# Turning the probabilities of two heads in four: on VectorE in squares of 32 with DMAs, in place of TensorE

## The chip, the cores and the metric

The kernel runs on one core of a Trainium2 chip. The metric is the time of one execution on the device in microseconds (us); below it, one profiled execution is read, in which every instruction of every engine has a start and a duration.

## The reference, cut to what matters

For 8 batches of 512 tokens with 512 features: causal attention with 16 query heads of 128 that share 4 key and value heads, a residual and a layer norm, then a mixture of 8 experts with the best two for each token, a residual and a layer norm. The change touches the attention alone:

```python
q = (x @ wq); k = (x @ wk); v = (x @ wv)          # 16, 4 and 4 heads of 128
scores = scale * q k^T, causally masked
p = exp(scores - row max);  p = p / row sum        # 512 x 512 per head, lower triangle
out = (p @ v) @ wo
x = layernorm(x + out)
```

The product p @ v contracts over keys, so TensorE needs p with the keys on the partitions. The scores come out with the queries there. So p must be turned, head by head.

## The kernel before, in words

The attention is a loop of 32 iterations: `it = 4 b + g`, batch b and key head g, each with the four query heads `n = 4 it` to `n + 3`. An iteration is of a kind: "first" (g = 0, it also makes the batch's values), "group" (g = 1, 2), and "batch" (g = 3, it also turns the next batch's x), or "end" for the last one of all. From the second batch on (`route` true) VectorE also works on the expert choice of a tile of 128 tokens of the batch before.

All engines run the iteration in an order written out by hand (`iteration` in `tensor`, `scalar`, `vector`, `gpsimd` and `sync`), with semaphores that only count up. Each engine is strictly in order, so a wait holds everything behind it. Every matrix product is done in three passes over a high and a low half of its operands; ScalarE copies a result out of PSUM as the high half, and VectorE subtracts this from the result to get the low half. For head n:

- TensorE makes the query (`query`, 12 matmuls) and the scores (`scores`, L1551).
- VectorE takes the scores out with mask and row maxima (`maxima`, L1937), ScalarE takes the exponentials (`exps`, L1824), VectorE inverts the sums (`inverse`, L1945), and GpSimd multiplies (`normalize`, L1423). The result is `probs`, two buffers of 128 x 1280 (the ten 128 x 128 squares on and under the diagonal).
- TensorE turns the ten squares into three PSUM banks (`transposes`, L1574), ScalarE copies these to `pT_hi` (L1834), VectorE makes `pT_lo` (L1948).
- TensorE multiplies with the values, two heads at a time (`values`), and the halves `oT_hi`, `oT_lo` are made by ScalarE and VectorE.
- `out_rows(t)` adds the four heads' part of output tile t, and VectorE's `add_rows` (L1976) takes it from PSUM.

TensorE's order in a group iteration: scores(n+1), out_rows 1 of the iteration before, query 2, turn head n, out_rows 2, turn head n+1, scores(n+2), query 3, out_rows 3, scores(n+3), values of heads n and n+1, key of the next iteration, turn head n+2, queries 0 and 1 of the next iteration, turn head n+3, scores(n+4), values of heads n+2 and n+3, out_rows 0. In a first iteration value rows stand in place of out_rows, and the key comes before the values. In a batch iteration two steps `turn_x` stand around out_rows 3.

out_rows 1 and 2 of a group or batch iteration use the same PSUM bank, so out_rows 2 waits for `add_rows` of tile 1 (the wait on `s_y_acc` in `out_rows`). The next iteration's query 0 goes to a bank of the values in group and batch iterations, so it waits until VectorE has made both low halves of the first pair of heads (`s_o_lo`). `transposes` waits on `s_pt_lo`, the count of units whose low half is done.

SyncE issues the loads of weights and the stores, also in a hand-written order; GpSimd issues the indirect DMAs. In batches 3 to 6 (job "split") a piece of the expert weights is loaded, split in halves and stored in each iteration, in two buffers in turn.

The diff changes `First.__init__`, `build`, `transposes` (L1565), `turn_x` (L1613), the `iteration` of four engines, ScalarE's and VectorE's `pT` (L1830, L1950), and SyncE's order; `piece_use` (L1116) goes.

Of the kernel before, what the change touches and what calls it, by code (L numbers as in the profile page):

```python
# [85 lines left out]
HALF = T // 2  # L86
RAW = HKV
# [408 lines left out]
class First:  # L496


    def __init__(self, arena, zone, wo_raw, v_hi, piece_raw, wo_last, sem):
# [3 lines left out]
        self.piece_hi = arena("piece_hi", [P, 2, NE, PIECE], F32R)  # L503
        self.v_raw = arena("v_raw", [P, TT, HKV * HD])
        self.piece_lo = arena("piece_lo", [P, 2, NE, PIECE], F32R)
        self.piece_raw = piece_raw("piece_raw", [P, 2, PIECE * NE])
# [21 lines left out]
def build(nc, x, wq, wk, wv, wo, gate_w, w_ffn, atoms, eaw, importance, mask_idx, out):  # L528
# [19 lines left out]
    with ExitStack() as top:  # L548
# [24 lines left out]
        def zone(at=0, size=None):  # L573
# [4 lines left out]
                  zone(42 * KB), zone(34 * KB), arena(16 * KB, 16 * KB), sem)  # L578
        E.place_early(zone(32 * KB))
        R.product.append(zone(32 * KB)("route_product_second", [P, DM]))  # L580
# [5 lines left out]
        tables = [Tables(arena(40 * KB, 8 * KB)), Rest(Space(nc, E.table_at, 8 * KB), Space(nc, gate_at, 4 * NE * DM))]  # L586
# [529 lines left out]
def piece_use(b, g):  # L1116

    return (b - SPLIT_BATCHES[0]) * (HKV // 2) + g // 2
# [28 lines left out]
def attention(nc, sem, s_passed, psum, ident, causal, upper, ones, R, F, E, N, table, row_i, entry_sum, y_acc, x_rows,  # L1147
# [35 lines left out]
    s_piece_in = [sem(f"piece_{k}_loaded") for k in range(2)]  # L1183
    s_piece_hi, s_piece_lo = sem("piece_hi_ready"), sem("piece_lo_ready")
    s_piece_out = [sem(f"piece_{k}_kept") for k in range(2)]
# [24 lines left out]
    def sync(sp):  # L1210
# [32 lines left out]
        def load_piece(b, g):  # L1243
            src = pieces[bass.ds(b - SPLIT_BATCHES[0], 1), g]
            sp.dma_start(F.piece_raw[:, g % 2], src.rearrange("a p n -> (a p) n")).then_inc(s_piece_in[g % 2], 16)

        def keep_piece(b, g):

            wait_apart(sp, s_piece_lo, piece_number(b, g) + 1, s_passed)
            for s, half in enumerate((F.piece_hi, F.piece_lo)):  # L1250
                dst = kept_pieces[bass.ds(b - SPLIT_BATCHES[0], 1), g, s]
                sp.dma_start(dst.rearrange("a p e r -> (a p) e r"), half[:, g % 2].bitcast(F32)
                             ).then_inc(s_piece_out[g % 2], 16)
# [47 lines left out]

        def iteration(b, g, it, kind, route, job):
            after, second = (g + 1) % HKV, (g + 2) % HKV
            if route and kind == "first":
# [34 lines left out]
            if not route:  # L1339
                keep_wo(it)  # L1340
            for j in range(3):
# [19 lines left out]
            if job == "last":  # L1361

                if g == 0:
                    for kept in s_piece_out:
                        sp.wait_ge(kept, 32 + 16 * PIECES)
# [30 lines left out]
    def gpsimd(pool):  # L1396
# [67 lines left out]
        def iteration(b, g, it, kind, route, job):  # L1464
# [65 lines left out]
            if job == "last" and g == 0:  # L1530
                for kept in s_piece_out:
                    pool.wait_ge(kept, 32 + 16 * PIECES)
# [11 lines left out]
    def tensor(pe):  # L1544
# [68 lines left out]
        def turn_x(b, chunks):  # L1613
            if 0 in chunks:

                pe.wait_ge(s_x_in, 16 * (b + 1))
                pe.wait_ge(s_pt_lo, 3 * (b * HKV * G - 2) + 3)
# [59 lines left out]
        def iteration(b, g, it, kind, route, job):  # L1677
# [29 lines left out]
            def turn_third():  # L1707
# [3 lines left out]
                transposes(n + 2, 0)  # L1711
# [18 lines left out]
            transposes(n, 0)  # L1730
# [5 lines left out]
            transposes(n + 1, 1)  # L1736
            scores(n + 2, 0)
# [17 lines left out]
            if kind in ("group", "batch"):  # L1755
# [15 lines left out]
            transposes(n + 3, 1)  # L1771
# [15 lines left out]
        def last_group(it, n, route):  # L1787
# [8 lines left out]
            transposes(n + 2, 0)  # L1796
            out_rows(3, it - 1, "spare", route)
            transposes(n + 3, 1)
# [16 lines left out]
    def scalar(act):  # L1815
# [14 lines left out]
        def pT(n, buf):  # L1830
            for u in range(3):
                a, z = UNIT[u]
                act.wait_ge(s_pt, 3 * n + u + 1)
# [19 lines left out]
        def high_piece(b, g, k):  # L1853
            act.wait_ge(s_piece_in[k], 16 * (piece_use(b, g) + 1))
            act.wait_ge(s_piece_out[k], 32 * (piece_use(b, g) + 1))
            act.copy(F.piece_hi[:, k], F.piece_raw[:, k].rearrange("p (r e) -> p e r", e=NE)).then_inc(s_piece_hi, 1)
# [17 lines left out]
        def iteration(b, g, it, kind, route, job):  # L1874
            n = it * G
            exps(n + 1, 1)
# [3 lines left out]
            pT(n, 0)  # L1880
# [620 lines left out]
```

## Time and profile before

| | |
|---|---|
| time, three runs | 1832.91 us median (1832.89 to 1837.29) |
| the profiled execution, its own time | 1834.23 us |
| its span, first to last instruction | 1832.4 us |
| mean granted TensorE clock | 0.990 of 2.4 GHz |
| TensorE busy (PE) | 97% of the span |
| VectorE (DVE), ScalarE (ACT), GpSimd (POOL) busy | 68%, 45%, 44% |
| DMA traffic | 317.93 MB, 174 GB/s mean |

A matmul's record is longer than what it costs in a row of matmuls, since they are pipelined; cost is read from start to start. The attention iterations take most of the span; the experts' tiles follow.

### The profile page before, as it was taken

How to read it: one execution, taken by the hardware profiler on the slowest of the kernel's cores; microseconds unless marked ns; L12 is line 12 of the kernel's file. 1: busy time of each engine (PE TensorE's matmuls, PEld its weight loads, DVE VectorE, ACT ScalarE, POOL GpSimd, SP SyncE). 2: the span in 40 equal slices, each digit the busy share in tenths (PEclk: the TensorE clock that was granted, in tenths of full speed). 3: DMA queues.
4: the chain of work that ended last, by engine and by line, in shares of the span. 5: the costliest groups of instructions: out<-in, count | busy, mean ns of one | idle time of the engine just before them, and what ended most of it. 6: DMA issues, size and time to landing. Idle time of an engine off the chain costs nothing.

```text
span 1832.4 us, 33342 instructions
## 1 busy us (share of the span) xinstructions
PE 1774.0 (97%) x9290; PEld 1501.4 (82%) x9290; DVE 1237.9 (68%) x3881; ACT 823.1 (45%) x2059; POOL 798.5 (44%) x1092
## 2 busy tenths in 40 slices
PE   8999999999999999999999999999999999999992
PEld 7888888888888888888888888888888888777872
DVE  5566467776777577857775777677776777763266
ACT  4444344444444444544454444444444443434454
POOL 6775344544454333323332333233323333676673
PEclk9999999999999999999999999999999999999996
DMA  9665443334333454454544444454435427654698
GB/s 329 227 223 196 161 145 116 116 111 168 116 116 110 150 156 159 147 172 144 162 151 159 136 150 155 154 175 159 158 122 196 150 93 308 220 173 152 230 341 335
DMA packets 157391, 317.93 MB, mean 174 GB/s; under 512 B 23088, under 2 KB 66256, under 8 KB 146704
## 3 DMA queue, kind: packets, MB, share of 16 engines
q1 hardware_dynamic: 138912, 275.83, 44.2%
q0 software_dynamic: 18288, 39.80, 7.0%
q8 instruction: 89, 1.46, 0.3%
q14 instruction: 102, 0.84, 0.1%
HBM read 227.30 MB, written 88.28 MB: 172 GB/s over the span
## 4 chain that ended last, share of the span: by engine, by line
PE 85%; DVE 5%; issue 3%; POOL 2%; DMA 2%; ACT 1%; DVEq 1%; ACTq 0%; POOLq 0%; SPq 0%
PE psum L1547 23%; PE psum L1549 23%; PE psum L1548 23%; PE psum L1574 7%; PE psum L2309 2%; PE psum L2310 2%; PE psum L2311 2%; PE psum L372 1%; DMA token_rows<-x,ids_now 1%; ACT probs L1824 1%; PE psum L794 1%; DVE pT_lo L1948 1%; POOL expert_weights L1443 1%; POOL probs L1423 0%; DVEq L384 0%
## 5 line engine op out<-in xcount | busy, mean ns | idle before, releaser
L1423 POOL TENSOR_SCALAR probs<-probs,row_inv 128x128 f32<-128x128 f32 (+3 forms) x512 | 308.0, 625 | 434.9 <-DVE row_inv L1945 433.0
L1824 ACT ACTIVATE probs<-probs,neg_max 128x512 f32<-128x512 f32 (+3 forms) x512 | 282.4, 554 | 361.5 <-DVE neg_max L1937 359.5
L1547 PE MATMUL psum<-xT_hi,w_hi 128*128 128x512 f32 x640 | 252.4, 394 | 0.7 <-DVE qT_lo L1962 0.7
L1937 DVE CUSTOM_DVE_ANT_0 probs<-psum,causal 128x512 f32<-128x512 f32 (+3 forms) x512 | 223.4, 487 | 42.8 <-issue 20.8
L1549 PE MATMUL psum<-xT_hi,w_lo 128*128 128x512 f32 x640 | 250.1, 391 | 0.0
L1548 PE MATMUL psum<-xT_lo,w_hi 128*128 128x512 f32 x640 | 249.7, 390 | 0.0
L1948 DVE TENSOR_TENSOR pT_lo<-psum,pT_hi 128x512 fp32r<-128x512 f32 (+1 forms) x384 | 206.5, 593 | 19.8 <-ACT pT_hi L1834 19.6
L1834 ACT CAST pT_hi<-psum 128x512 fp32r<-128x512 f32 (+1 forms) x384 | 172.3, 526 | 65.1 <-PE psum L1574 65.1
L1547 PE MATMUL psum<-wo_hi,oT_hi 128*128 128x512 f32 x496 | 196.8, 397 | 0.0
L1549 PE MATMUL psum<-wo_hi,oT_lo 128*128 128x512 f32 x496 | 193.9, 391 | 0.0
L1548 PE MATMUL psum<-wo_lo,oT_hi 128*128 128x512 f32 x496 | 193.4, 390 | 0.0
L1547 PE MATMUL psum<-kT_hi,qT_hi 128*128 128x512 f32 (+3 forms) x512 | 173.4, 339 | 0.0
L1574 PEld LDWEIGHTS psum<-ident,probs 128*128 128x128 f32 x1280 | 145.8, 141 | 27.0 <-DVE pT_lo L1948 11.9
L1574 PE MATMUL psum<-ident,probs 128*128 128x128 f32 x1280 | 161.5, 273 | 4.5 <-DVE pT_lo L1948 4.3
L1548 PE MATMUL psum<-kT_lo,qT_hi 128*128 128x512 f32 (+3 forms) x512 | 165.6, 323 | 0.0
L1549 PE MATMUL psum<-kT_hi,qT_lo 128*128 128x512 f32 (+3 forms) x512 | 165.0, 322 | 0.0
L1962 DVE SCALAR_TENSOR_TENSOR qT_lo<-psum,qT_hi 128x512 fp32r<-128x512 f32 x128 | 88.4, 691 | 103.6 <-ACT qT_hi L1838 99.5
L1401 POOL CAST v_hi<-v_raw 128x512 fp32r<-128x512 f32 x32 | 27.4, 856 | 296.5 <-PE psum L1549 281.0
L1838 ACT ACTIVATE qT_hi<-psum 128x512 fp32r<-128x512 f32 x128 | 76.3, 596 | 163.8 <-PE psum L1549 161.5
L1549 PEld LDWEIGHTS psum<-xT_hi,w_lo 128*128 128x128 f32 x640 | 120.2, 188 | 25.5
L1547 PE MATMUL psum<-pT_hi,v_hi 128*128 128x512 f32 (+1 forms) x384 | 140.0, 365 | 0.5 <-DVE neg_max L1937 0.4
L1547 PEld LDWEIGHTS psum<-xT_hi,w_hi 128*128 128x128 f32 x640 | 120.2, 188 | 24.4 <-DVE qT_lo L1962 0.9
(251 smaller groups left out, 3869.5 us busy)
## 6 DMA issues: line engine op xcount, KB each, us to landing
w_hi<-split_qk_weights SPq DMA_DIRECT2D x140, 256.0 KB, 2.7
w_lo<-split_qk_weights SPq DMA_DIRECT2D x140, 256.0 KB, 3.0
wo_hi<-split_out_weights SPq DMA_DIRECT2D x27, 1024.0 KB, 5.4
wo_lo<-split_out_weights SPq DMA_DIRECT2D x27, 1024.0 KB, 7.7
expert_weights_hi_lo<-split_expert_weights SPq DMA_DIRECT2D x8, 2048.0 KB, 9.7
x_in<-in_L_attn_x_dram SPq DMA_DIRECT2D x8, 1024.0 KB, 6.6
expert_weights<-fill SPq DMA_DIRECT2D x16, 512.0 KB, 5.0
attn_residual<-y_acc SPq DMA_DIRECT2D x8, 1024.0 KB, 4.7
```

The source lines that it names most:

```text
L1423: last = pool.tensor_scalar(p, p, row_inv[:, buf, i:i + 1], 1.0, ALU.mult, ALU.mult)
L1547: pe.matmul(dst, hi_s, hi_m, start=start, stop=False)
L1548: pe.matmul(dst, hi_s, lo_m, start=False, stop=False)
L1549: return pe.matmul(dst, lo_s, hi_m, start=False, stop=stop)
L1574: last = pe.transpose(psum[:, BANKS_PT[unit], at:at + P], probs[:, buf, src:src + P], ident[:])
L1824: last = act.activation(probs[:, buf, a:a + w], probs[:, buf, a:a + w], ACT.Exp, bias=neg_max[:, buf, i:i + 1], scale=-1.0, accum_out=row_ ...
L1834: act.copy(pT_hi[:, buf, a:z], psum[:, BANKS_PT[u], 0:z - a]).then_inc(s_pt_hi, 1)
L1838: act.mul(qT_hi[:, buf], psum[:, bank, :], SCALE).then_inc(s_q_hi, 1)
L1937: last = dve.tensor_tensor_reduce(probs[:, buf, a:a + w], psum[:, BANK_S + bank, col:col + w], causal[:, T - w:T], -1.0, -MASKED, ALU.add, ...
L1948: dve.tensor_tensor(lo, src, hi.bitcast(F32), ALU.subtract).then_inc(done, 1)
L1962: dve.scalar_tensor_tensor(out=qT_lo[:, buf], in0=psum[:, bank, :], scalar=SCALE, in1=qT_hi[:, buf].bitcast(F32), op0=ALU.mult, op1=ALU.su ...
L2309: pe.matmul(dst, hi_of(j, c), hi, start=c == 0, stop=False)
```

## The change

In the 27 iterations with `route` whose kind is not "end" (7 first, 14 group, 6 batch), heads n and n+2 ("moved" heads, k = 0 and 2) are no longer turned by TensorE. VectorE turns `probs` in squares of 32 x 32 within their partitions into `F.blocks` (five instructions, 1280 columns). Then SyncE issues 16 DMAs, each with 32 partitions of 320 columns (1280 bytes), which carry the squares to their partitions in `F.moved`. ScalarE copies `F.moved` to `pT_hi` in one instruction of 1280 columns, and VectorE subtracts for `pT_lo` in one. The order on TensorE, ScalarE and VectorE is changed in these iterations, the key comes ahead of the values in group iterations too, and `transposes` of head n+3 waits for the low halves of three heads of its iteration. The expert pieces have one buffer in place of two, and a few buffers lie elsewhere. In the other five iterations the order stays.

```diff
+def is_moved(kind, route):
+    return route and kind != "end"
+def turned_number(it, k, kind, route):
+    if not route:
+        return it * G + k
+    return MOVED_FROM * G + 2 * (it - MOVED_FROM) + (k if kind == "end" else k // 2)
+def lows_done(n, k, kind, route):
+    if is_moved(kind, route):
+        return 3 * (n + (1, 0, 2, 3)[k]) + 3
+    return 3 * (n + k) + 3
@@ sync @@
+        def move(it, k, free):
+            wait_apart(sp, s_blocks, moved_number(it, k) + 1, s_passed)
+            wait_apart(sp, s_pt_lo, free, s_passed)
+            for i in range(SIDE):
+                for j in range(SIDE):
+                    sp.dma_start(F.moved[j * SQUARE:(j + 1) * SQUARE, i], F.blocks[i * SQUARE:(i + 1) * SQUARE, j]
+                                 ).then_inc(s_moved, 16)
         def iteration(b, g, it, kind, route, job):
+            if is_moved(kind, route):
+                move(it, 0, 3 * n)
             if route and kind == "first":
...
             if not route:
                 keep_wo(it)
+            if is_moved(kind, route):
+                move(it, 1, 3 * (n + 2) + 3)
             for j in range(3):
                 slot(j, it + 2, second)
@@ tensor @@
-        def transposes(n, buf):
-            pe.wait_ge(s_norm, n + 1)
-            pe.wait_ge(s_pt_lo, 3 * n + 3)
+        def transposes(n, k, kind, route):
+            buf = k % 2
+            pe.wait_ge(s_norm, n + k + 1)
+            pe.wait_ge(s_pt_lo, lows_done(n, k, kind, route))
...
-            transposes(n, 0)
+            moved = is_moved(kind, route)
+            if not moved:
+                transposes(n, 0, kind, route)
...
                 filler(1 if kind == "first" else 2)
-            transposes(n + 1, 1)
-            scores(n + 2, 0)
+            if moved:
+                scores(n + 2, 0)
+            transposes(n, 1, kind, route)
+            if not moved:
+                scores(n + 2, 0)
...
-            if kind == "batch":
-                turn_x(b + 1, (0, 1))
+            if kind == "batch" and not moved:
+                turn_x(b + 1, (0, 1), route)
             filler(3)
             if kind == "batch":
-                turn_x(b + 1, (2, 3))
+                turn_x(b + 1, (0, 1) if moved else (2, 3), route)
             scores(n + 3, 1)
-            if kind == "first":
+            if kind == "batch" and moved:
+                turn_x(b + 1, (2, 3), route)
+            key_first = kind == "first" or moved and kind == "group"
+            if key_first:
                 pe.wait_ge(s_q_lo, n + 4)
                 key(it + 1)
             values_first()
...
             query(1, it + 1, bank_of_query(1, kind))
-            transposes(n + 3, 1)
+            transposes(n, 3, kind, route)
             scores(n + 4, 0)
@@ scalar @@
+        def moved_pT(n, it, k):
+            act.wait_ge(s_moved, 16 + 16 * SIDE * SIDE * (moved_number(it, k) + 1))
+            act.wait_ge(s_o, n + 2 * k)
+            act.copy(pT_hi[:, 0].rearrange("p (b i c) -> p b i c", i=SIDE, c=SQUARE),
+                     F.moved[:].rearrange("p i (b c) -> p b i c", c=SQUARE)).then_inc(s_pt_hi, 3)
...
             if kind == "first":
                 v(b, 3)
+            if moved:
+                moved_pT(n, it, 0)
             if kind == "batch":
-                high_xT(act, F, psum, b + 1, range(C), BANKS_PT[:2])
+                high_xT(act, F, psum, b + 1, range(C // 2) if moved else range(C), BANKS_PT[:2])
             exps(n + 3, 1)
+            if kind == "batch" and moved:
+                high_xT(act, F, psum, b + 1, range(C // 2, C), BANKS_PT[:2])
...
                 qT(n + 5, 1, bank_of_query(1, kind))
+            if moved:
+                moved_pT(n, it, 1)
@@ vector @@
+        def turn_blocks(n, it, k):
+            dve.wait_ge(s_norm, n + 2 * k + 1)
+            dve.wait_ge(s_moved, 16 + 16 * SIDE * SIDE * moved_number(it, k))
...
+            for i in range(TT):
...
+                last = dve.transpose(blocks[:, at[0]:at[-1] + 1:3], src)
...
+            dve.transpose(blocks[:, at:at + 1], src).then_inc(s_blocks, 1)
+        def moved_pT(n, k):
+            dve.wait_ge(s_pt_hi, 3 * (n + 2 * k) + (6 if k == 0 else 3))
+            view = "p (b i c) -> p b i c"
+            low(pT_lo[:, 0].rearrange(view, i=SIDE, c=SQUARE), pT_hi[:, 0].rearrange(view, i=SIDE, c=SQUARE),
+                F.moved[:].rearrange("p i (b c) -> p b i c", c=SQUARE), s_pt_lo, 3)
...
             maxima(n + 1, 1)
+            if moved:
+                turn_blocks(n, it, 0)
...
                 qT(n + 3, 1, BANK_A)
+            if moved:
+                moved_pT(n, 0)
             if late:
                 route_logits(dve, R, tt, (1, 2), products)
...
             if kind not in ("first", "end"):
                 add_rows(it - 1, 3, "group")
             if kind == "batch":
+                low_xT(dve, F, psum, b + 1, (0, 1) if moved else (2, 3), BANKS_PT[:2])
+            if moved:
+                turn_blocks(n, it, 1)
+            maxima(n + 3, 1)
+            if kind == "batch" and moved:
                 low_xT(dve, F, psum, b + 1, (2, 3), BANKS_PT[:2])
-            maxima(n + 3, 1)
...
-            if kind == "first":
+            if key_first:
                 kT(it + 1)
...
                 qT(n + 5, 1, bank_of_query(1, kind))
-                pT(n + 3, 1)
+                if moved:
+                    moved_pT(n, 1)
+                pT(n, 3, moved)
                 maxima(n + 4, 0)
```

## Rows read from the trace of the kernel before

**Rows 1.** The page: busy time, and the chain that ended last, by engine

```profile
PE 1774.0 (97%) x9290; PEld 1501.4 (82%) x9290; DVE 1237.9 (68%) x3881; ACT 823.1 (45%) x2059; POOL 798.5 (44%) x1092
...
PE 85%; DVE 5%; issue 3%; POOL 2%; DMA 2%; ACT 1%; DVEq 1%; ACTq 0%; POOLq 0%; SPq 0%
```

**Rows 2.** Timeline of TensorE, a group iteration: start us, us, operation

```profile
513.29 1.25 PE L1574 MATMUL psum<-ident,probs 128*128 128x128 f32 x10
514.29 0.48 PE L1547 MATMUL psum<-wo_hi,oT_hi 128*128 128x512 f32 x1
...
516.90 0.39 PE L1549 MATMUL psum<-wo_hi,oT_lo 128*128 128x512 f32 x1
517.96 1.31 PE L1574 MATMUL psum<-ident,probs 128*128 128x128 f32 x10 [0.67 <-DVE pT_lo L1948]
...
526.49 0.39 PE L1547 MATMUL psum<-kT_hi,qT_hi 128*128 128x512 f32 x1
...
531.87 0.39 PE L1547 MATMUL psum<-xT_hi,w_hi 128*128 128x512 f32 x1
...
535.63 0.48 PE L1547 MATMUL psum<-xT_hi,w_hi 128*128 128x512 f32 x1
...
541.17 1.25 PE L1574 MATMUL psum<-ident,probs 128*128 128x128 f32 x10
```

**Rows 3.** Timeline of VectorE, same iteration

```profile
510.59 0.69 DVE L1937 CUSTOM_DVE_ANT_0 probs<-psum,causal 128x512 f32<-128x512 f32 x1
511.21 0.08 DVE L1937 DVE_READ_ACCUMULATOR2_ANT neg_max<- 128x1 f32 x1
...
511.90 0.42 DVE L1937 CUSTOM_DVE_ANT_0 probs<-psum,causal 128x256 f32<-128x256 f32 x1
...
512.24 0.69 DVE L680 BATCH_NORM_STATS2 route_stats<-route_rows 128x6 f32<-128x512 f32 x1
...
513.48 0.68 DVE L1976 TENSOR_TENSOR y_acc<-psum,y_acc 128x512 f32<-128x512 f32 x1
...
527.52 0.69 DVE L1937 CUSTOM_DVE_ANT_0 probs<-psum,causal 128x512 f32<-128x512 f32 x1
...
529.36 0.69 DVE L698 CUSTOM_DVE_ANT_0 route_product<-route_rows,route_gate 128x512 f32<-128x512 f32 x1
```

**Rows 4.** Timeline of ScalarE, same iteration, then a first iteration

```profile
530.63 0.57 ACT L1846 CAST oT_hi<-psum 128x512 fp32r<-128x512 f32 x1
...
541.37 0.60 ACT L1838 ACTIVATE qT_hi<-psum 128x512 fp32r<-128x512 f32 x1 [2.13 <-PE psum L1549]
...
628.84 0.59 ACT L1860 COPY v_raw<-psum 128x512 f32<-128x512 f32 x1 [2.12 <-PE psum L1549]
```

**Rows 5.** Groups by shape, VectorE then ScalarE: count, busy, mean ns

```profile
L1948 DVE TENSOR_TENSOR piece_lo<-piece_raw,piece_hi 128x1024 fp32r<-128x1024 f32 x16 | 35.2, 2203 | 0.0
...
L1996 DVE TENSOR_TENSOR wv_lo<-wo_raw,wv_hi 128x2048 fp32r<-128x2048 f32 x1 | 2.3, 2286 | 0.0
...
L1856 ACT CAST piece_hi<-piece_raw 128x1024 fp32r<-128x1024 f32 x16 | 36.6, 2288 | 0.0
...
L1868 ACT CAST wv_hi<-wo_raw 128x2048 fp32r<-128x2048 f32 x1 | 1.9, 1912 | 0.0
```

**Rows 6.** Timeline of SyncE's queue, at the start and in the group iteration

```profile
12.63 1.16 SPq L1216 DMA_DIRECT2D split_qk_weights<-w_hi  x1
...
526.74 0.32 SPq L1240 DMA_DIRECT2D wo_hi<-split_out_weights  x1
```

**Rows 7.** The page: DMA issues, KB each, us to landing

```profile
route_rows<-attn_residual SPq DMA_DIRECT2D x30, 256.0 KB, 3.4
```

**Rows 8.** Busy by window, 2 us each; PEclk after the five engines

```profile
28.00:30.00 2.00, 2.00 (x10) 1.95 (x9) 1.21 (x5) 0.70 (x2) 1.52 (x3) 0.53 1.07 389
30.00:32.00 2.00, 2.00 (x8) 1.73 (x8) 1.94 (x7) 1.25 (x7) 1.43 (x2) 0.61 1.09 383
```

**Rows 9.** Timeline of TensorE, at the start

```profile
23.89 3.64 PE L952 MATMUL psum<-eawT,atoms_sb 128*128 128x16 f32 x32
```

More of the change, by code:

```diff
@@ L1710, in turn_third @@
                 pe.wait_ge(s_o_lo, n + 1)
-                transposes(n + 2, 0)
+                if not is_moved(kind, route):
+                    transposes(n, 2, kind, route)
             scores(n + 1, 1)
@@ L1754, in iteration @@
             values_first()
-            if kind in ("group", "batch"):
+            if not key_first:
                 pe.wait_ge(s_q_lo, n + 4)
@@ L1875, in iteration @@
             n = it * G
+            moved = is_moved(kind, route)
             exps(n + 1, 1)
@@ L1879, in iteration @@
             qT(n + 2, 0, BANK_A)
-            pT(n, 0)
+            if not moved:
+                pT(it, 0, kind, route)
             if kind == "first":
@@ L1884, in iteration @@
                 qT(n + 3, 1, BANK_A)
-            pT(n + 1, 1)
-            exps(n + 2, 0)
+            if moved:
+                exps(n + 2, 0)
+            pT(it, 1, kind, route)
+            if not moved:
+                exps(n + 2, 0)
             if kind == "first":
@@ L1904, in iteration @@
                 oT(n, 0, kind)
-                if kind in ("group", "batch"):
+                if not key_first:
                     kT(it + 1)
-                pT(n + 2, 0)
+                if not moved:
+                    pT(it, 2, kind, route)
             if kind != "end":
@@ L2007, in iteration @@
             quads = QUADS_OF[g] if not route and g < len(QUADS_OF) else ()
+            moved = is_moved(kind, route)
+            key_first = kind == "first" or moved and kind == "group"
             maxima(n + 1, 1)
+            if moved:
+                turn_blocks(n, it, 0)
             if not route and kind == "first":
@@ L2020, in iteration @@
             qT(n + 2, 0, BANK_A)
-            pT(n, 0)
+            if not moved:
+                pT(n, 0, moved)
             if kind == "end":
@@ L2052, in iteration @@
                 qT(n + 3, 1, BANK_A)
+            if moved:
+                moved_pT(n, 0)
             if late:
                 route_logits(dve, R, tt, (1, 2), products)
-            if kind == "batch":
+            if kind == "batch" and not moved:
                 low_xT(dve, F, psum, b + 1, (0, 1), BANKS_PT[:2])
@@ L2074, in iteration @@
             if kind == "end":
-                pT(n + 2, 0)
+                pT(n, 2, moved)
             if route:
@@ L2088, in iteration @@
                 count_later(dve, N, upper, q)
-            if kind in ("group", "batch"):
+            if not key_first and kind != "end":
                 kT(it + 1)
-            if kind != "end":
-                pT(n + 2, 0)
+            if kind != "end" and not moved:
+                pT(n, 2, moved)
             if route:
```

111 lines of the change are left out of this document (64 added, 47 removed).

## The prediction

> **What bounds the kernel now.** First the busy times and the chain on the page: TensorE is busy 97% of the span, and 85% of the chain lies on it [rows 1]. So the time is TensorE's order, instruction by instruction, and what counts is whether a step of its order goes or a wait comes into it. Second the timelines of one group iteration, read from start to start. On TensorE the ten squares of head n take 513.29 to 514.29, 1.00 us. Before the next ten stands a gap: the last of the 12 matmuls of out_rows 2 starts at 516.90 and costs some 0.23, the turning starts at 517.96, so 0.83 us are idle for `pT_lo` [rows 2]. All else follows without a gap. Third the other engines' timelines, for what they do while TensorE runs on: they are not the bound, but some hand-overs have nearly no slack. The one to see is y_acc: VectorE ends add_rows of tile 1 at 513.48 + 0.68 = 514.16, and out_rows 2, which waits for it, starts at 514.29 [rows 2, 3]. What hides this wait today is the turning of head n, which the change takes away.
>
> **What is removed.** 27 iterations x 2 heads x 1.00 us = 54 us of TensorE's order. The gap of 0.83 us goes too, since it waited for the low halves of head n; I count it in the 20 group and batch iterations: 17 us. Together 71 us. ScalarE's and VectorE's three copies from PSUM per moved head go as well, which is worth nothing by itself, since neither engine is the bound; it becomes one copy each.
>
> **Prices of what is added.** No VectorE turning is in the trace. Nearest are VectorE's passes of one element a step: 512 columns take 0.62 us to the next start, 256 take 0.34 [rows 3], so 1.09 ns a column and 0.06 us an instruction. Five instructions with 1280 columns: 1.40 + 0.30 = 1.7 us, which I take. The low end is 1.4 us (the columns alone; no row shows more than one element a step), the high end the dearest copy of the trace, piece_lo with 2.20 us for 1024 strided columns [rows 5], that is 2.75. The Trainium skill (VectorE: DVE Perf Modes, The three transpose paths) gives 311 ns for one 128 x 128 in bf16 on VectorE; ten of these would be 3.1 us, an estimate from that page, and by it the forecast would stand some 66 us higher.
>
> ScalarE's copy of 1280 columns from SBUF: wv_hi took 1.91 us for 2048 [rows 5], so 1.25 us; high end piece_hi, 2.29 for 1024, so 2.86. VectorE's subtraction with both operands in SBUF: wv_lo took 2.29 for 2048 [rows 5], so 1.45; high end 2.75. Both moved patterns have runs of 32 columns, nearer to wv than to the piece's strides.
>
> The 16 DMAs: an issue takes SyncE 0.32 us in the iterations and 1.16 at the start, where the queues are full [rows 6]. With the step to the next I take 0.4 x 16 = 6.4 us, and 2.6 more to the landing of the last (low end 0; 3.4 is the landing of a 256 KB load [rows 7]). High end 1.16 x 16 = 18.6.
>
> **Three new waits on TensorE.** I go through the order with these prices.
>
> *Wait A, before the turning of head n+3, in all 27.* `transposes` there waits for three heads' low halves, the second moved head's among them. That head's copy stands on ScalarE behind qT(n+5), the high half of the query that TensorE has just made, and its subtraction on VectorE behind that. In the trace, query 1 hands over at 541.17 and ScalarE starts at 541.37 for 0.60 us [rows 2, 4]. So TensorE waits 0.20 + 0.60 + 1.25 + 1.45 = 3.5 us, where before it went on at once. Nothing behind it makes this good: scores(n+4) and the values come later by as much, since pT of head n+3 follows the turning as before. 27 x 3.5 = 95 us.
>
> *Wait F, before out_rows 2, in 20 (group, batch).* With head n's turning gone, TensorE wants out_rows 2 at 513.29. VectorE has the first turning of squares, 1.7 us, ahead of the route variance and add_rows 1, so that ends at 514.16 + 1.7 = 515.9: a wait of 2.65 us. 20 x 2.65 = 53 us. SyncE's first 16 DMAs run beside this: issued by about 520.4 and landed by 523, and ScalarE wants them at about 525.
>
> *Wait B, behind the values of the first pair.* Let T be the start of scores(n+3), 526.49 before. Before, maxima(n+3) started at T + 1.0, ended at T + 2.9 and ScalarE was through with the exponentials at T + 4.1 [rows 2 to 4]. After, VectorE does in order: low half of the third query (done about T - 0.3), the moved subtraction 1.45, add_rows 3, 0.6, the second turning of squares 1.7, and starts maxima at T + 3.5; exponentials end at T + 6.6. Then the inverse, a logit pass of 0.65, kT_lo, oT_lo, a logit pass, oT_lo, 0.6 each: T + 9.85. TensorE's scores and values take 531.87 - 526.49 = 5.4, the key 2.75 (half of 541.17 - 535.63) [rows 2], and it wants query 0 at T + 8.15. Wait 1.7 us; before, the key and the turning of head n+2 covered this. x 14 = 24 us. In a batch iteration the second half of xT is split only behind the late maxima, about T + 9.35 against TensorE at T + 7.3 for the key, and 0.3 remain later: 2.35 x 6 = 14 us. In a first iteration the moved copy stands on ScalarE behind the last value row, 628.84 + 0.5 in the trace [rows 4], which is T + 0.7 with T the start of scores; the subtraction ends at T + 3.5, two logit passes and the turning put maxima at T + 6.5, and kT_lo is done at T + 11.5 against T + 8.15: 3.4 x 7 = 24 us.
>
> SyncE's second 16 DMAs start at about T + 3.5 (T + 6.5 in a first iteration), behind 2 MB of output weights in group and batch ones, and land at about T + 12.5 (T + 15.5); ScalarE wants them at about T + 16 (T + 17.5). Covered, at nothing; without the cover it is wait A that grows by what is late. The loads of weights behind the moves have most of an iteration to land, and are also at nothing. So are the single piece buffers: the stores are issued at the end of an iteration and the next copy comes at the end of the next. The experts' part is untouched.
>
> **Sum.** Group: -2.0 - 0.83 + 2.65 + 1.7 + 3.5 = +5.0. Batch: -2.83 + 2.65 + 2.35 + 3.5 = +5.7. First: -2.0 + 3.4 + 3.5 = +4.9. 14 x 5.0 + 6 x 5.7 + 7 x 4.9 = +138.5 us. On the profiled execution's 1834.2 this gives 1972.7; that execution lies 1.3 us above the median of 1832.9, so I forecast 1971 us. By the bounds: a microsecond more of turning costs 47 us (once in 7 iterations, twice in 20), one of ScalarE's copy 34 (A, and B in first ones), one of subtraction 54. Low end of the turning: -14. High ends: turning +49, copy +55, subtraction +70.
>
> **Rivals.**
> - *Dearer copies or squares*, at piece rates: up to 1971 + 174 = 2145. For: the only copies of the trace with a rearranged pattern cost twice. Against: wv and the maxima. Chance 0.13, half of it under 2075.
> - *The clock.* The one dip in the trace: from 28 to 32 us the mean granted clock is 0.53 and 0.61, so mostly the lower level (1.2 GHz) [rows 8], behind 3.6 us of products of 16 columns [rows 9]. In these 4 us it gave 2.3 us of full speed, so it cost 1.7. If each wait A brought one, 27 x 1.7 = 46: 2017 us. For: 3.5 us of nothing and 1 of turning are like that stretch. Against: one such place is thin ground. The Trainium skill (TensorE: Matmul & The Clock Gate, Part 1) says that the array falls to 1.2 GHz after an idle stretch. By it this case would be met at least in part. Chance 0.09.
> - *SyncE is late*: issues at 1.16 us. Each move lands some 12 us later; after the slack of 2 to 4 us that is about +9 for either move, and up to 27 x 18 = 486. At 0.7 us an issue it is about +3 for either, 2130. Against: the rows in the iterations. Chance 0.05.
> - *Only wait A*: VectorE catches up, F and B don't show. -71 + 95 = +24, 1857 us. Chance 0.07.
> - *Faster*: one mechanism at one place, wait A, with both copies at two columns a step, and F and B hidden. A is then 0.20 + 0.60 + 0.63 + 0.73 = 2.2 us: -71 + 58, 1820 us. It decides from A under 2.6 us on. Against: no row shows a rate over one, and A follows from the order of three engines. Chance 0.04.
>
> **How the numbers follow.** The sum as it stands has 0.62. The predicted time is its 1971. The range 1895 to 2075 takes in the sum with its bounds, the clock and half of the dearer case, and stops short of the others, 0.2 in all. A measurement of this kernel can tell about 0.3% from no change. Slower by more than that: all but the last two rivals' low parts, 0.94; within 0.3%: 0.02; faster: 0.04.
>
> **What would show it.** TensorE's waits should list its turning of `probs` behind DVE pT_lo, about 3.5 us each, 27 times; out_rows 2 behind DVE y_acc, 2.6 us, 20 times; projections behind DVE oT_lo, kT_lo or xT_lo, 2 to 3 us. TensorE busy near 88%. Five transposes on VectorE should sum to 1.7 us, and a move's 16 issues to 6.4. I am wrong if TensorE's wait before head n+3 is under 2 us, if ScalarE's moved copies are released by a DMA rather than following at once, or if a group iteration comes out less than 3 us longer than before.

## The result, and the profile after

The changed kernel takes 2099.1 us (median of 4 runs, 2095.2 to 2103.1) where the kernel before takes 1833.2: a ratio of 1.144 [1.143, 1.146]. The forecast was 1971 us with a range that ended at 2075. So the sign was right and the size was not: 266 us were added where the sum had 138.5.

The page of the kernel after, busy times and the chain, answering to [rows 1]:

```profile
span 2101.3 us, 33626 instructions
PE 1818.5 (87%) x8750; PEld 1512.5 (72%) x8750; DVE 1329.7 (63%) x4043; ACT 819.4 (39%) x1951; POOL 849.1 (40%) x1092
...
PE 47%; DVE 20%; issue 12%; ACT 8%; SPq 5%; POOL 3%; DMA 3%; DVEq 1%; ACTq 0%; POOLq 0%
```

TensorE lost 540 of its instructions and is busy *longer*: 1818.5 us against 1774.0. That is the first thing to see. 54 us of turning went, so its remaining work should take 1720; it takes 98 us more. The rest of the loss is waiting. TensorE's waits after (us in total, times, longest):

```profile
PE psum L1616 <- DVE pT_lo L2020: 93.1, 27, 3.5
PE psum L1588 <- DVE y_acc L2071: 50.8, 20, 2.8
PE psum L1588 <- DVE oT_lo L2020: 42.6, 20, 5.2
PE psum L1588 <- DVE qT_lo L2057: 28.6, 22, 4.8
PE psum L1588 <- DVE xT_lo L789: 13.8, 6, 2.3
```

The first line is wait A, the second wait F, the last three wait B and what came with it: 229 us. By the kind of the iteration, from TensorE's timeline: behind the values of a group iteration, of a batch iteration (two steps), then a first iteration (scores of head n+3, then behind the values):

```profile
364.99 0.47 PE L1588 MATMUL psum<-xT_hi,w_hi 128*128 128x512 f32 x1 [2.11 <-DVE oT_lo L2020]
...
418.44 0.49 PE L1588 MATMUL psum<-xT_hi,w_hi 128*128 128x512 f32 x1 [2.30 <-DVE xT_lo L789]
421.69 0.47 PE L1588 MATMUL psum<-xT_hi,w_hi 128*128 128x512 f32 x1 [0.25 <-DVE oT_lo L2020]
...
704.70 0.49 PE L1588 MATMUL psum<-kT_hi,qT_hi 128*128 128x512 f32 x1 [1.18 <-DVE qT_lo L2057]
717.18 0.79 PE L1588 MATMUL psum<-xT_hi,w_hi 128*128 128x512 f32 x1 [3.93 <-DVE oT_lo L2020]
```

So 2.1, 2.55 and 5.1 us stand in these iterations where the sum had 1.7, 2.35 and 3.4. Over all of a kind the means are 2.6 (group, with some 0.4 us before scores of head n+3), 2.3 (batch) and 4.7 (first). The timeline of TensorE in a group iteration, behind wait B (L1588, 2.11 us idle) and at the turning behind wait A:

```profile
540.53 0.39 PE L1590 MATMUL psum<-pT_hi,v_lo 128*128 128x512 f32 x1
543.03 0.77 PE L1588 MATMUL psum<-xT_hi,w_hi 128*128 128x512 f32 x1 [2.11 <-DVE oT_lo L2020]
543.60 0.63 PE L1589 MATMUL psum<-xT_lo,w_hi 128*128 128x512 f32 x1
544.02 0.63 PE L1590 MATMUL psum<-xT_hi,w_lo 128*128 128x512 f32 x1
544.45 0.63 PE L1588 MATMUL psum<-xT_hi,w_hi 128*128 128x512 f32 x1
...
546.45 0.40 PE L1590 MATMUL psum<-xT_hi,w_lo 128*128 128x512 f32 x1
546.68 0.39 PE L1588 MATMUL psum<-xT_hi,w_hi 128*128 128x512 f32 x1
546.91 0.39 PE L1589 MATMUL psum<-xT_lo,w_hi 128*128 128x512 f32 x1
...
553.69 2.39 PE L1616 MATMUL psum<-ident,probs 128*128 128x128 f32 x10 [3.44 <-DVE pT_lo L2020]
555.73 0.77 PE L1588 MATMUL psum<-kT_hi,qT_hi 128*128 128x512 f32 x1
```

Read the starts. For 3.1 us behind the wait two matmuls of 512 columns stand 0.43 us apart, then 0.23: first the lower of the clock's two levels (1.2 GHz), then the upper (2.4). Ten squares behind wait A take 2.04 us to the next start, against 1.00 before [rows 2]. The granted clock of the whole span is 0.943, against 0.990: of 2101.3 us, 120 us of full speed were not granted, against 18 before.

The prices of the new work: VectorE's turning, ScalarE's copy, VectorE's subtraction (groups of instructions with shapes kept apart), and SyncE's queue in a first iteration:

```profile
L2032 DVE STREAM_TRANSPOSE probs_blocks<-probs 128x384 f32<-128x384 f32 x108 | 53.8, 536 | 0.0
L2032 DVE STREAM_TRANSPOSE probs_blocks<-probs 128x128 f32<-128x128 f32 x54 | 16.7, 309 | 11.5 <-POOL probs L1465 11.2 <-DVE route_logits L704 0.2
L1885 ACT CAST pT_hi<-probs_moved 128x1280 fp32r<-128x1280 f32 x54 | 67.9, 1257 | 7.1 <-DMA probs_moved<-probs_blocks 7.1
L2020 DVE TENSOR_TENSOR pT_lo<-probs_moved,pT_hi 128x1280 fp32r<-128x1280 f32 x54 | 81.2, 1503 | 16.4 <-ACT pT_hi L1885 16.4
```

```profile
686.96 10.29 SPq L1337 DMA_DIRECT2D probs_moved<-probs_blocks  x16
697.87 0.35 SPq L633 DMA_DIRECT2D route_rows<-attn_residual  x1
```

The 16 issues take 10.3 us, not 6.4, and in a first iteration the load of the route's rows stands behind them.

### The profile page after: what moved, and what is told of

Same layout as the page of the kernel before. It is cut to its first block, busy times and chain, and to the rows that moved or that the text cites. A ratio compares the mean times of both kernels' runs of the same rounds, so it can differ in the third digit from the quotient of the medians.

```text
span 2101.3 us, 33626 instructions
## 1 busy us (share of the span) xinstructions
PE 1818.5 (87%) x8750; PEld 1512.5 (72%) x8750; DVE 1329.7 (63%) x4043; ACT 819.4 (39%) x1951; POOL 849.1 (40%) x1092
## 4 chain that ended last, share of the span: by engine, by line
PE 47%; DVE 20%; issue 12%; ACT 8%; SPq 5%; POOL 3%; DMA 3%; DVEq 1%; ACTq 0%; POOLq 0%
PE psum L1588 12%; PE psum L1590 12%; PE psum L1589 12%; ACT probs L1875 5%; SPq L1337 5%; PE psum L1616 4%; DVE pT_lo L2020 3%; POOL probs L1465 3%; DVE probs_blocks L2032 3%; PE psum L2419 2%; ACT pT_hi L1885 2%; PE psum L2421 2%; PE psum L2420 2%; DVE probs L2009 2%; DVE y_acc L2071 2%
## 5 line engine op out<-in xcount | busy, mean ns | idle before, releaser
L1465 POOL TENSOR_SCALAR probs<-probs,row_inv 128x128 f32<-128x128 f32 (+3 forms) x512 | 355.2, 708 | 491.5 <-DVE row_inv L2017 488.6
L1588 PE MATMUL psum<-xT_hi,w_hi 128*128 128x512 f32 x640 | 269.8, 422 | 56.4 <-DVE oT_lo L2020 42.0
L1590 PE MATMUL psum<-xT_hi,w_lo 128*128 128x512 f32 x640 | 263.2, 411 | 0.0
L1589 PE MATMUL psum<-xT_lo,w_hi 128*128 128x512 f32 x640 | 263.1, 411 | 0.0
L1588 PE MATMUL psum<-wo_hi,oT_hi 128*128 128x512 f32 x496 | 200.0, 403 | 50.8 <-DVE y_acc L2071 50.8
L1588 PE MATMUL psum<-kT_hi,qT_hi 128*128 128x512 f32 (+3 forms) x512 | 185.4, 362 | 27.9 <-DVE qT_lo L2057 27.9
L1616 PE MATMUL psum<-ident,probs 128*128 128x128 f32 x740 | 116.8, 316 | 93.1 <-DVE pT_lo L2020 93.1
L1588 PEld LDWEIGHTS psum<-xT_hi,w_hi 128*128 128x128 f32 x640 | 128.9, 201 | 93.5 <-DVE oT_lo L2020 50.0
L2020 DVE TENSOR_TENSOR pT_lo<-psum,pT_hi 128x512 fp32r<-128x512 f32 (+1 forms) x222 | 121.8, 596 | 100.6 <-ACT pT_hi L1893 100.5
L1616 PEld LDWEIGHTS psum<-ident,probs 128*128 128x128 f32 x740 | 101.2, 164 | 107.0 <-DVE pT_lo L2020 92.7
L1588 PEld LDWEIGHTS psum<-wo_hi,oT_hi 128*128 128x128 f32 x496 | 95.2, 192 | 77.7 <-DVE y_acc L2071 35.9
L1589 PEld LDWEIGHTS psum<-xT_lo,w_hi 128*128 128x128 f32 x640 | 129.5, 202 | 25.9
```

Source lines behind the costliest of these rows:

```text
L1465: last = pool.tensor_scalar(p, p, row_inv[:, buf, i:i + 1], 1.0, ALU.mult, ALU.mult)
L1588: pe.matmul(dst, hi_s, hi_m, start=start, stop=False)
L1589: pe.matmul(dst, hi_s, lo_m, start=False, stop=False)
L1590: return pe.matmul(dst, lo_s, hi_m, start=False, stop=stop)
L1616: last = pe.transpose(psum[:, BANKS_PT[unit], at:at + P], probs[:, buf, src:src + P], ident[:])
L2020: dve.tensor_tensor(lo, src, hi.bitcast(F32), ALU.subtract).then_inc(done, count)
```

## Experiments

The theories. *Waits and clock*: of the 266 us, some 170 are the waits less the work removed, and the remaining 95 are TensorE's clock, which falls at the waits. Its rival: TensorE's matmuls are longer for another reason (what VectorE, ScalarE and the DMAs do beside them), so that only the waits count. And for each wait: is it the order of one engine's work (can be mended), or has that engine no room?

**1. The waits filled** (`e1_fill`). In waits F, B and A stand matmuls that nobody reads:

```
+        def fill(bank, buf, count):
+            for _ in range(count):
+                pe.matmul(psum[:, bank, :], qT_hi[:, buf, 0:P], qT_hi[:, buf], start=True, stop=True)
...
+                fill(BANKS_PT[0], 1, 10)     (F)
...
+                fill(BANKS_PT[0], 1, 8)      (B)
...
+                fill(BANKS_PT[0], 0, 12)     (A)
```

In F and A a wait on TensorE for an earlier hand-over stands ahead of the filling; in batch iterations B's stands ahead of the key.

> The changed kernel with matmuls of 512 columns that nobody reads, put into TensorE's new waits: 10 before out_rows 2 in group and batch iterations, 8 ahead of query 0 (of the key in a batch iteration), 12 ahead of the turning of head n+3. At 0.23 us each they are shorter than the waits (2.5, 2.1 and 3.44 us), so they cost nothing by themselves. Theory (the clock): TensorE's new idle stretches bring its granted clock to the lower level behind them, and this is the 95 us that the waits do not explain; with the gaps filled the mean granted clock returns to 0.98 or more and the time falls by 60 to 95 us, to 2005 to 2040. Rival (no clock): the missing 95 us are longer waits and contention, and the time stays at 2099 within 6 us.

2034.1 us, ratio 1.109 [1.107, 1.111], granted clock 0.984. Its page: 

```profile
PE 1908.5 (94%) x9490; PEld 1586.6 (78%) x9490; DVE 1327.8 (65%) x4043; ACT 818.7 (40%) x1951; POOL 843.0 (41%) x1092
```

740 more matmuls, 169 us of work at 0.228 each, and the kernel is 65 us *faster*. TensorE's busy time less the filling is 1740, within 20 us of its work. Only TensorE's own activity was changed, so what went is the clock's: 65 us of time, 78 of the 98 by the busy time, and by the granted clock 87 of the 102 us of full speed that had been lost over before ((1 - 0.984) x 2032.6 = 33 are left, against 120). For these the rival is out; for the last 20 us of busy time it is not tested.

**2. Which wait brings the clock down.** Only A filled (`e9_fill_a`), and only F and B (`e11_fill_fb`).

> The kernel after with 12 unread matmuls of 512 columns in wait A alone (before the turning of head n+3, 27 times); the waits before out_rows 2 and behind the values stay empty. Theory (each wait brings a stretch at the lower clock, A's about 1.8 us each): of the 98 us by which TensorE's busy time is longer than its work, 50 go, since the kernel with head n+2 alone, which has wait A and hardly another, has 50 of them and the one with head n alone, with the others, 33: 2045 to 2060 us, and the kernel with all three filled keeps another 15 to 25 us ahead of it. Rival (the clock falls behind the other waits as well whatever stands in A): 2080 to 2100.

> The kernel after with unread matmuls in the waits before out_rows 2 and behind the values, and wait A left empty: the complement of e9. All three filled gave 65 us, A alone about 20 (by the ratios). If each wait has a lower-clock stretch of its own, the rest is 45: ratio 1.115 to 1.123. If one wait's stretch stands in for another's, so that only filling all of them helps, it is 10 to 25: ratio 1.130 to 1.139.

A alone: 2093.3 us, ratio 1.134 [1.131, 1.137], so 20 us less than after by the ratio (the kernel before took 1846.5 us beside this run, which is why ratios are compared). F and B alone: 2086.4 us, 1.138 [1.136, 1.140], 13 us less. The first missed the theory's 2045 to 2060 and came out as its rival had it; the second is where "one stands in for another" had put it. 20 and 13 don't make 65. The timeline of TensorE behind wait F says why, in the same iteration of both kernels. Filled at A (first fence), and after, where nothing is filled (second):

```profile
569.66 0.51 PE L1588 MATMUL psum<-wo_hi,oT_hi 128*128 128x512 f32 x1 [2.67 <-DVE y_acc L2079]
...
570.83 0.63 PE L1588 MATMUL psum<-wo_hi,oT_hi 128*128 128x512 f32 x1
571.25 0.63 PE L1589 MATMUL psum<-wo_lo,oT_hi 128*128 128x512 f32 x1
```

```profile
574.98 0.50 PE L1588 MATMUL psum<-wo_hi,oT_hi 128*128 128x512 f32 x1 [2.68 <-DVE y_acc L2071]
575.32 0.39 PE L1589 MATMUL psum<-wo_lo,oT_hi 128*128 128x512 f32 x1
575.55 0.40 PE L1590 MATMUL psum<-wo_hi,oT_lo 128*128 128x512 f32 x1
```

With A filled, this wait F is followed by a stretch at the lower level (0.43 us from start to start); with A empty, a wait as long is not. A wait is counted here where the granted clock falls during it or before the next wait of a microsecond. So counted, it falls at 5 of the 20 waits F in after and at 18 of 20 with A filled; at 22 of the 27 waits A in after and at 24 of 27 with F and B filled. In the six batch iterations of after it falls at exactly one of the two, the wait for `xT_lo` or wait A. One wait's stretch stands in for another's. So the cost can't be handed out wait by wait, and filling some of them gave 13 or 20 us where filling all gave 65. What decides at which wait it comes stays open.

**3. Wait A undone by its cause** (`e2_two_lows`). The turning of head n+3 waits for two heads' low halves and no longer for the second moved head's:

```
-        return 3 * (n + (1, 0, 2, 3)[k]) + 3
+        return 3 * (n + (1, 0, 2, 2)[k]) + 3
```

> The turning of head n+3 waits for two heads' low halves, not three, so that it no longer waits for the second moved head. Theory (wait A is the chain from query 1 over ScalarE's two passes and VectorE's subtraction): that chain now ends before the values instead, with VectorE's three subtractions for head n+3 behind it: some 5.1 us after query 1, of which the turning and the scores cover 3.1. The wait of 3.44 becomes one of 2.0, and with less idle time there is less of the lower clock: 27 x 1.4 = 38 us and up to 30 more, 2030 to 2061. Rival: the values give all of it back, 2099.

2046.0 us, 1.114 [1.111, 1.117], inside the 2030 to 2061 expected. The wait goes on to the values, where the same low half is wanted next, and is 54.4 us instead of 93.1: 39 us less waiting and, with the clock, 53 less in all. Wait A was what the prediction took it for.

**4. One DMA for the 16** (`e3_one_dma`). It leaves the squares in their partitions, so the products of the moved heads are not the reference's; the counts that wait for the DMAs follow, all else stays.

```
-            for i in range(SIDE):
-                for j in range(SIDE):
-                    sp.dma_start(F.moved[j * SQUARE:(j + 1) * SQUARE, i], F.blocks[i * SQUARE:(i + 1) * SQUARE, j]
-                                 ).then_inc(s_moved, 16)
+            sp.dma_start(F.moved[:], F.blocks[:]).then_inc(s_moved, 16)
```

> One DMA of 128 x 1280 in place of the 16 of a move. The squares then stay in their partitions, so the products of the two moved heads are not those of the reference; all waits and all bytes are as before. Theory (SyncE's issue time): 16 issues take 10.3 us of SyncE, not 6.4, which holds the load of the route rows in a first iteration; VectorE waits for them, and TensorE for the low half of the query (28.6 us in 22 waits). With one issue these waits go: 7 x 4 = 28 us and up to 15 of clock behind them, 2056 to 2075; ScalarE's 7.1 us of waits for the moved squares go too. Rival: the carrying itself is late or contends everywhere, and 60 us or more go. Second rival: the issue time is hidden, 2099.

2098.9 us, 1.144 [1.142, 1.146]: the same as after. TensorE's waits:

```profile
PE psum L1613 <- DVE pT_lo L2017: 93.1, 27, 3.5
PE psum L1585 <- DVE oT_lo L2017: 65.0, 27, 5.7
...
PE psum L1585 <- DVE qT_lo L2054: 7.1, 15, 1.1
```

The wait for `qT_lo` falls by 21.5 us and the one for `oT_lo` grows by 22.4. SyncE's time is covered by wait B: whichever of the two comes first, VectorE ends at the same place. My expectation missed, the second rival (the issue time is hidden) held.

**5. One head at a time.** Only head n moved (`e4_head_n`), only head n+2 moved (`e5_head_n2`), the other turned by TensorE as before. In e4 the key stands behind the values again in group iterations, and in e5 the orders around head n are those of the kernel before; in short:

```
-                move(it, 1, 3 * (n + 2) + 3)           (e4; in e5 the first move goes)
...
-                if not is_moved(kind, route):
-                    transposes(n, 2, kind, route)
+                transposes(n, 2, kind, route)          (e5: the same for head n)
```

> Head n alone is moved; head n+2 is turned by TensorE as in the kernel before, and the key stands behind the values in group iterations. Wait A has no cause here. Theory (waits add up as in the prediction): 27 us of turning saved, wait F 51 us, the query's wait in first iterations 28 us, wait B covered by the turning of head n+2 and the key: 1833 - 27 + 51 + 28 = 1885, and up to 20 us of clock: 1880 to 1905. Rival (each moved head costs alike, by its DMAs and copies): half of 266, 1966.

> Only the second moved head, head n+2, is turned by VectorE; head n stays on TensorE, and the orders of TensorE, VectorE and ScalarE around head n are those of the kernel before. The kernel after has 266 us more than before; the one with head n alone has 93. Theory (each moved head costs its own waits and the lower clock behind them): 27 x 1.0 us of turning are removed, wait A (TensorE's turning of head n+3 behind pT_lo) stays at 27 x 3.4 = 93, wait F (y_acc before out_rows 2) is gone, the waits behind the values stay at some 10 to 40, the clock costs 40 us: 1833 - 27 + 93 + 25 + 40 = 1964, range 1940 to 1985, granted clock 0.97. Rival (the waits only appear together, since both heads share the one buffer and SyncE's queue; one head alone loses little, wait A shrinks under 2 us as the move has a whole iteration): 1850 to 1900.

Head n: 1926.7 us, 1.052 [1.050, 1.054]. Head n+2: 1966.8 us, 1.073 [1.071, 1.075]. The first keeps F (49.2 us) and 29.7 for `qT_lo` and loses A; the second keeps A (`pT_lo`, 98.1) and 26.1 for `oT_lo` and loses F. By TensorE's busy time over its work, some 33 and 50 us are the clock's (the second read in an execution of 1979.6 us, 13 above the median). In the second its 14 waits of 1.45 us for `oT_lo` were never followed by the lower level, wait A at 22 of 27. Together they add 93 + 133 = 226 of the 266. The first came out above its expectation, since I had left at most 20 us for the clock; the second, with 40 for it, met its own.

**6. The turning later on VectorE** (`e6_late_turn`), behind add_rows 1 and the inverse, against wait F:

```
-            if moved:
+            if moved and kind == "first":
                 turn_blocks(n, it, 0)
...
             inverse(n + 1, 1)
+            if moved and kind != "first":
+                turn_blocks(n, it, 0)
```

> The kernel after with VectorE's first turning of squares placed behind add_rows of tile 1 and the inverse, in group and batch iterations (20). Theory: the wait before out_rows 2 is made by this order alone, so it falls from 2.5 to about 0.9 us, -33 us; qT_lo of the third query comes later and gives back up to 18 of it; the clock gains some us where the wait was: 2065 to 2085 us. Rival (VectorE's work is on the path anyway, so that whatever is moved ahead of the turning only moves the wait to scores of head n+2): 2095 to 2105, with y_acc's wait gone and qT_lo's grown by the same.

2117.2 us, 1.155 [1.153, 1.157]: slower than after, and above both ranges. Wait F shrinks from 50.8 to 19.3 us as expected, and the gain is more than given back: `oT_lo` +24, `qT_lo` +10, `xT_lo` +6. ScalarE's copy of the moved head shows by what:

```profile
L1885 ACT CAST pT_hi<-probs_moved 128x1280 fp32r<-128x1280 f32 x54 | 67.9, 1257 | 64.0 <-DMA probs_moved<-probs_blocks 63.9
```

7.1 us of waiting for the DMA became 63.9. The first move had next to no cover: 2 us later, its 10 us of issues set the time of ScalarE's copy and, behind that, of `oT_lo` (66.7 instead of 42.6). I had it landed 2 us ahead of ScalarE's need; at 0.64 us an issue those 2 us are gone, and it was nearly in time in the change's own order alone.

**7. Head n alone, with orders of its own.** `e7_head_n_ordered` puts add_rows 1 ahead of the turning and the inverse and the query's low half right behind it, VectorE's maxima of head n+3 ahead of the moved subtraction, SyncE's load of the route's rows ahead of the move, and TensorE's turning of x where it was before; ScalarE's moved copy stays ahead of the exponentials of head n+3 and the key ahead of the values in group iterations. The main part:

```
+            if moved and kind != "first":
+                add_rows(it - 1, 1, "group")
             if moved:
                 turn_blocks(n, it, 0)
+                inverse(n + 1, 1)
+                qT(n + 2, 0, BANK_A)
```

> Only head n is turned by VectorE, and the orders are made so that no wait should be left: on VectorE add_rows of tile 1, the inverse and the query's low half stand as early as before or earlier around the turning of squares, the maxima of head n+3 go ahead of the moved subtraction, on ScalarE the moved copy goes ahead of the exponentials of head n+3, and the batch iteration's turning of x stands as before. Theory (TensorE's time is the bound, and the waits come from where the other engines' new work was put): 27 us of TensorE are removed, the waits for y_acc and qT_lo (79 us in the kernel with head n alone and the orders of the change) fall under 20 in all, with that the clock is back at 0.985 or more: 1815 to 1845 us, perhaps under the 1833.9 of before. Rival (VectorE and ScalarE have no room for one more copy and turning in the stretch between scores n+1 and the first pair's values, wherever it is put): the waits come back at pT_lo or oT_lo, 1870 to 1920 us.

1901.1 us, 1.036 [1.035, 1.038]: the theory's 1815 to 1845 missed. The waits for `y_acc` and `qT_lo` fell from 79 us to 5, 16.4 for `pT_lo` came, mostly before the values of batch iterations, and one came that neither theory had: GpSimd's normalising of head n+1, 38.8 us in 20 iterations. On GpSimd's queue the route's rstd stands ahead of it, and that waited for VectorE's route variance, which I had put behind the turning. `e8_pool_order` turns these two round on GpSimd and puts the key ahead of the values in batch iterations too:

```
-            if route and kind != "first":
+            if route and kind == "end":
+                route_rstd(pool, R, it - TT)
             normalize(n + 1, 1)
+            if route and kind in ("group", "batch"):
+                route_rstd(pool, R, it - TT)
```

> The kernel of e7 (head n alone on VectorE, its orders rearranged) with two more changes of order: GpSimd normalises head n+1 ahead of the route's rstd in group and batch iterations (in e7 it waited for the route variance, which VectorE does behind the turning of squares, and TensorE waited 20 times for it, 38.8 us), and in a batch iteration the key goes ahead of the values, as in the others (there TensorE waited 2.7 us for the moved head's pT_lo, 16.4 us). Theory (every wait left is a matter of order, and the lower clock goes with the waits): 55 us of waits go, up to 15 come back at pT_lo or qT_lo as all is tight there, and of the 35 us of clock some 20 to 25 go: 1825 to 1845 us. Rival (VectorE's chain around the turning of squares is too long for the place, so that the waits return elsewhere): 1860 to 1890.

1897.7 us where the kernel before took 1846.5, ratio 1.027 [1.025, 1.029]: the theory missed again, and its rival (the waits return elsewhere) held. The wait moved on by one step: 36.8 us for `qT_lo` of the fourth query, behind three logit passes. `e10_query_early` puts it ahead of them:

```
+            if moved and early:
+                inverse(n + 2, 0)
+                qT(n + 3, 1, BANK_A)
             if early:
                 route_logits(dve, R, tt, (1,), products)
```

> The kernel of e8 with the fourth query's low half and the inverse of head n+2 put ahead of three logit passes on VectorE, in group and batch iterations. In e8 the wait for the probabilities of head n+1 had gone and came back 2 us later as one for qT_lo before scores of head n+3 (2.5 us, 15 times, 36.8 us), behind these passes. Theory (still a matter of order): that wait falls under 10 us in all, the clock gives back about 10 more: ratio to before 1.000 to 1.012, so 1834 to 1856 us where before takes 1834. Rival (no slack is left anywhere: the wait returns at pT_lo before the values or at kT_lo): 1.022 to 1.028.

1859.4 us, 1.013 [1.011, 1.015], granted clock 0.986. Its waits on TensorE:

```profile
PE psum L800 <- DVE pT_lo L2014: 15.5, 6, 2.6
PE psum L1588 <- DVE pT_lo L2014: 11.6, 15, 1.5
PE psum L1588 <- DVE qT_lo L2051: 9.8, 15, 0.9
...
PE psum L1588 <- DVE oT_lo L2014: 6.9, 21, 0.7
```

Its working closes: 1832.4 - 27 of turning + 44 of waits + 14 of TensorE's busy time over its work = 1863, and its span is 1858.7. It stands a thousandth above the theory's upper end (1.012). And it doesn't beat the kernel before: even one head, with the best orders that I found, costs more in waits (44 us) than the 27 us that TensorE saves. No version that I ran is faster than the kernel before. Whether a batch iteration that leaves both heads on TensorE (15.5 us of the waits) would bring this one level with it wasn't tried.

## Why the prediction was right or wrong

**Right.** TensorE's order bounds, and each wait is where the order of three engines put it. *Wait A*: 93.1 us, 27 times; the forecast was 95. *Wait F*: 50.8 us, 20 times; 53. *Prices*: squares 1.67 us a head from their first start to the next instruction's (571.37 to 573.04 in VectorE's timeline; the durations in the fence overlap, so they aren't added) against 1.7; copy 1.257 against 1.25; subtraction 1.503 against 1.45. *What was costed at nothing*: weights, stores and pieces don't show among TensorE's waits. The Trainium skill's figure for one 128 x 128 on VectorE (VectorE: DVE Perf Modes, The three transpose paths), which is for bf16, weighed as 3.1 us a head, would have been wrong for this shape: an instruction of 128 columns of f32 takes 309 ns here, about the page's 311, but one of 384 takes 536, and five cover a head.

**Wrong: one term left out, and sizes:**

- *The clock*, some 95 us against none. This is the step that failed: the sum put TensorE's clock at nothing. I had it as a rival at 46 us and a chance of 0.09, from one dip of the trace before [rows 8, 9], which I called thin ground. Its price of 1.7 us a time was about right: behind wait B in the fence above the starts from 543.03 to 546.45 are 3.42 us apart for eight matmuls, 1.6 more than at 0.228 each; behind wait A the ten squares take 1.04 more and the two matmuls behind them 0.45. But I gave it to A alone. With two such stretches in each of 27 iterations it would be 27 x 3.1 = 84 us, an estimate from this one iteration; and it comes at F too, as experiment 2 shows. The dip was not the only one of its kind in the trace before, either. There is another behind a wait of 1.26 us and four products of 8 columns (starts 0.43 us apart):

```profile
1645.07 0.39 PE L664 MATMUL psum<-route_chosen,upper 128*128 128x8 f32 x2 [1.26 <-DVE route_chosen L722]
...
1646.66 0.63 PE L2311 MATMUL psum<-expert_weights_hi_lo,tokT_lo 128*128 x1
1647.09 0.63 PE L2309 MATMUL psum<-expert_weights_hi_lo,tokT_hi 128*128 x1
```

The Trainium skill (TensorE: Matmul & The Clock Gate, HAM oscillation) describes a kernel whose array fell to the lower clock at the DMA wait of some 3 to 5 us ahead of each of its tiles. Wait A here, 3.44 us, agrees at 22 of 27; but the clock fell at 15 of 17 waits of 1.6 us and more for `oT_lo` as well, most of them 2.1 us. The clock should have been part of the sum and not a rival: a forecast of 7 to 8.5 us of waits in each iteration was at the same time a forecast of the waits' clock.
- *Wait B*, 85 us against 62. Group iterations have 36.6 us of it against 24, first ones 33.0 against 24, batch ones 14.0 against 14. In a first iteration the route's rows come behind SyncE's 16 issues, VectorE waits for them (1.96 us in the one shown), and scores of head n+3 wait for `qT_lo`, 21.4 of the 33.0 us. But experiment 4 takes that away and `oT_lo` is late instead, 33.1 us in these iterations, so SyncE is not what sets it. Which of VectorE's steps there I had too short was not taken apart. In a group iteration two waits were in no term. Some 0.35 us stand before scores of head n+3, for `qT_lo` of the fourth query (1.05 in the last two): 6.5 us in all. And VectorE's second turning of squares waits for GpSimd's normalising of head n+2, 0.65 us in the iteration shown and 11.2 us in all (the fence of prices): there the maxima of head n+3 start 4.2 us behind its scores, where I had 3.5.
- *The gap of 0.83 us*, 17 us counted as saved and about 5 got. In the trace before the wait for `pT_lo` ahead of the second turning shows in 7 iterations only, 4.3 us in all. I had read one iteration's timeline [rows 2] and multiplied by 20; the view of waits had the count.
- *An issue*, 0.645 us against 0.4. At 0.7 I had written +3 us for either move, 2130 us in all, as a rival. The issue came near that and its cost did not: wait B hid it, and experiment 4 takes it away for nothing.

The sum again with what came: 138.5 - 4 (A, F) + 23 (B) + 12.5 (the gap) = 170, and 95 to 98 for the clock: 265 to 268, against 266. The 95 is what is left over and the 98 is TensorE's busy time over its work; experiment 1 shows 65 to 78 of it to be the clock's.

## What to carry to other kernels

- Where one engine runs 97% busy, new waits of 2 to 3.5 us on it cost more than themselves: here some 95 us of lower clock came with 229 of waits. A sum that has such waits must have the clock as a term.
- Moving work off the bounding engine pays only if none of its results comes back to that engine's order late; here 54 us were taken off and 229 of waits came. Each mended order showed the next wait (`y_acc`, then GpSimd, then `qT_lo`, then `pT_lo`): follow the chain through all queues before the first edit.
- A size read off one iteration is to be multiplied by the count in the view of waits, not by the number of iterations.

## What the runs showed of the hardware

- At idle stretches of 2.1 to 3.4 us on TensorE between runs of dense matmuls the clock often fell to the lower level for about 3 us, but not each time: at 5 of 20 waits F in after, at 18 of 20 with A filled, at none of 14 waits of 1.45 us with head n+2 alone. What decides is open.
- A matmul whose result nobody reads, put into a wait, made the kernel faster: with 169 us of such work it took 65 us less.
- SyncE took 0.63 to 0.71 us for an issue of a DMA over 32 partitions (10.0 to 11.4 us for 16), where most over 128 partitions take 0.32 to 0.43, and the one of `e3_one_dma` 0.48.
- GpSimd's normalising took 708 ns in mean against 625 before (718 with head n alone, 623 with head n+2 alone). What slows it was not tried.
- Beside the runs of `e8_pool_order` and `e9_fill_a`, on another chip than the rest, the kernel before took 1846.5 us and not 1833. Their traces have it in the experts' part, whose orders no experiment touches: 313.0 and 311.4 us behind the last turning, against 296.8 in the trace before.
